# Order of the engines' work in four stages of a decoder megakernel, four buffers of expert weights, a mask product in bf16

## The chip, the cores and the metric

One core of a Trainium2 chip runs the whole program in one launch. The metric is the device time in microseconds (us). The kernel before was timed in three runs: median 4763.19, from 4760.88 to 4769.77.

## The reference

`reference()` is a decoder of four layers on `x` 32 x 128 x 128 (32 sequences of 128 tokens and 128 columns; the kernel calls a sequence a block). Each layer adds three functions of the normalised `x` to it: a self attention, a cross attention and a feed forward. The change touches four of the twelve. Cut to what matters:

```
# second self attention (L1): heads of 8 columns, 16 heads; S = 128 tokens
q, k, v = split(x @ Wproj + bproj)
Z   = k @ W0 per head
dz1 = vjp(layernorm at Z)(y1 - v)                  # the "gradient", per head and token
Z2  = Z - tril(k k^T) @ dz1;  dz2 = vjp(layernorm at Z2)(y2 - v)
ctx = q @ W0 - tril(q k^T) @ (dz1 + dz2)
ctx = group norm of ctx over tokens and columns of a head;  return ctx @ Wout + bout

# third cross attention (L2), its first part, the modulation: 128 tokens on 120 keys, 4 heads
scores = q k^T / sqrt(32), -inf where vision_mask is off
topv = top_k(scores, 32); probs = softmax(topv) scattered back
c = mean over heads(probs) @ V * text_mask
film = c @ W_film + b_film                         # scales and shifts, in and out
x = layernorm(x) * (1 + gate * scale_in) + gate * shift_in

# last self attention (L3): 16 heads of 64 columns, causal
normed = x / |x| * sqrt(dim) * gamma;  q, k, v = split(normed @ w_qkv)
return softmax(causal(q k^T / 8)) @ v @ w_out

# last feed forward (L3): product keys, 4 heads, 512 experts, 8 chosen per head
q = x @ W_q; sim = q . keys (two halves of 64 keys);  sx, sy = top_8 of each half
scores, indices = top_8(sx + sy)
w = silu((x . down_embed[indices]) * softmax(scores));  experts = sum w * up_embed[indices]
return silu(x @ W_up) @ W_down + experts
```

## The kernel before

`x` stays in SBUF for the whole program as 128 x 32 x 128 (`R.x`). Twelve stages follow each other, each a `phase` with its own buffers, PSUM tiles and semaphores. In a stage each engine (VectorE `dve`, ScalarE `act`, TensorE `pe`, GpSimd, SyncE for DMA) runs its own list of instructions, written by hand; nothing is reordered later. Engines meet through semaphores: `then_inc(s.name_ready, 1)` at a producer, `wait_ge(s.name_ready, b + 1)` at a consumer. A wait holds back everything behind it on the same engine, so the order in which an engine's list is written is part of the schedule.

The lists are software pipelines. `skewed(eng, depth, n, per)` (L180) yields rounds; in round t the code under `item(lag)` works on block (or pair of blocks) t - lag. `halved` (L201) does the same over half-blocks of eight heads. The first and last rounds are written out, those between run in a loop (`Fori`) of `per` rounds.

- **Second self attention**, `l1_attn` (L1046), 16 pairs of blocks, depth 3. A round: the normalised pair `xhat` (VectorE, L1150), its transpose `xT` (TensorE L1280, copied by ScalarE L1210), the projections `projected(b, 0)` and `projected(b, 1)` (TensorE), squares of `z` and of two later quantities (ScalarE, L1229 for the first), their reductions (VectorE L1176, L1179, L1182), the gradients, many products of TensorE, and for pair b - 3 the group norm, the transposes of ctx into `p_c`, the copy `cT` (ScalarE L1213), the output product (TensorE L1294), the sum into `x` (VectorE L1170) and the statistics of the new `x`.
- **Modulation**, `l2_film` (L2039), 32 blocks, depth 3. A round of TensorE: transpose of `xhat` (L2198), k, q and V products into `p_a`, the sum over heads of the transposed weights into `p_m` (L2209, from eight diagonal matrices `diag` that ScalarE makes at L2165 and L2166), the mask (L2215: ones times `mneg`, a row of 0 and -1e30 in a 128 x 32 x 120 f32 tile that is zero but for its first partition) and the scores into `p_s` (L2218), c (L2222), and at the end the film products L2228 to L2230. ScalarE copies film and `xr` (L2158, L2159), makes `xT`, the diagonals, the Exp and the other copies. VectorE picks the top 32 with MAX8 and match_replace.
- **Last self attention**, `l3_attn` (L2500), 64 half-blocks, depth 5. Two PSUM tiles are shared between steps: `p_x` holds by turns the heads' outputs (`av`, L2615), v, and xT; `p_y` holds q, then k (`projected`, L2602), then once per block the output projection (L2657). VectorE copies qT (L2549), eT and kT (L2558) and adds the projection to `x`.
- **Last feed forward**, `l3_ffn` (L2827), 16 pairs, depth 3. `w` holds for each pair, two rows of tokens and four heads the 512 expert weights: Exp of the sums (ScalarE L2954), times the dot products of `x` with `down` and cut to the chosen (VectorE L2904, L2911), silu (ScalarE, `silus`, L2921 and L2922; the chosen-again ones in `e_c` are summed into `rest`), the last one corrected by `added` (VectorE L2864), the sum over heads and the transpose in one go (TensorE L2979, 16 products per row of tokens), the copy `wT` (ScalarE L2940), and the product with `up` (TensorE L2991). Beside it the dense path: up (L2970), hT (ScalarE L2931), down (L2988). `w`, `sums`, `cand`, `hT` have two buffers (PER2 = 2).

## Time and profile before

The profiled execution took 4762.61 us, of which its span is 4760.8. TensorE ran at a mean granted clock of 0.812.

| | us | PE | DVE | ACT | PEclk |
|---|---|---|---|---|---|
| whole span | 4760.8 | 3486.1 | 2834.1 | 1788.2 | 0.81 |
| second self attention, 826.23 to 1385.43 | 559.20 | 314.37 | 466.45 | 65.53 | 0.73 |
| modulation, 2090.97 to 2557.13 | 466.16 | 368.50 | 294.27 | 246.62 | 0.65 |
| last self attention, 3369.99 to 3962.88 | 592.89 | 498.44 | 367.97 | 264.72 | 0.97 |
| last feed forward, 4240.03 to 4760.80 | 520.77 | 360.79 | 353.39 | 307.35 | 0.86 |

Columns PE, DVE and ACT are the busy us of TensorE, VectorE and ScalarE in the stretch. PEclk is the share of its full clock that TensorE was granted. A stretch's windows tell how full each engine is, the timeline tells in which order an engine did its work and which wait stood before it. GpSimd and the DMA queues do next to nothing in these four stages.

### The profile page before, as it was taken

What the parts mean: (1) busy time and instruction counts of PE and PEld (TensorE: products, weight loads), DVE (VectorE), ACT (ScalarE), POOL (GpSimd) and SP (SyncE); (2) the same over time, 40 slices, a digit from 0 to 9 for tenths busy, and PEclk for the clock granted to TensorE, in tenths of its full rate; (3) what the DMA queues carried; (4) which work ended last, traced back from release to release, by engine and by line L of the source; (5) the groups of instructions that cost most, each with busy time, mean ns of one, the idle gap of its engine ahead of it and who ended that gap; (6) DMA issues with size and microseconds to landing.
All of it is one profiled execution on the core that took longest, in us unless ns stands there. A gap on an engine that the chain in (4) does not pass through costs nothing. (4 is left out here: it accounts for less than half of the span.)

```text
span 4760.8 us, 71373 instructions
## 1 busy us (share of the span) xinstructions
PE 3486.1 (73%) x22142; PEld 2515.3 (53%) x22143; DVE 2834.1 (60%) x8335; ACT 1788.2 (38%) x5180; POOL 676.2 (14%) x867
## 2 busy tenths in 40 slices
PE   3576396555548858558888859999688887867776
...
DMA packets 111452, 152.49 MB, mean 32 GB/s; under 512 B 21594, under 2 KB 88216, under 8 KB 109718
## 3 DMA queue, kind: packets, MB, share of 16 engines
...
q14 instruction: 59, 0.48, 0.0%
...
## 5 line engine op out<-in xcount | busy, mean ns | idle before, releaser
L1245 PE MATMUL l_attn_p_s<-l_attn_outer,l_attn_upper 128*128 128x512 f32 x256 | 182.3, 877 | 201.9 <-DVE l_attn_outer L1190 121.4
L95 POOL TENSOR_TENSOR rstd<-vareps,minus_half 128x32 f32<-128x32 f32 x11 | 59.8, 5439 | 1527.9 <-DVE vareps L86 1393.6
L398 ACT ACTIVATE l_ffn_sg<-l_ffn_p_g 112x512 f32<-112x512 f32 x192 | 114.6, 597 | 391.9 <-PE l_ffn_p_g L378 368.5
L2582 ACT ACTIVATE l_attn_E<-l_attn_p_s,l_attn_nm 128x128 f32<-128x128 f32 x512 | 182.3, 382 | 157.6 <-DVE l_attn_nm L2545 157.6
L409 DVE TENSOR_TENSOR l_ffn_h<-l_ffn_sg,l_ffn_p_u 112x512 f32<-112x512 f32 x192 | 131.8, 687 | 172.7 <-PE l_ffn_p_u L381 172.1
L1245 PEld LDWEIGHTS l_attn_p_s<-l_attn_outer,l_attn_upper 128*128 128x128 f32 x256 | 70.2, 288 | 302.3 <-issue 178.7
L2979 PE MATMUL l_ffn_p_w<-ident,l_ffn_w 128*128 128x128 f32 x1024 | 157.0, 326 | 89.0 <-DVE l_ffn_w L2864 76.1
L381 PE MATMUL l_ffn_p_u<-l_ffn_f_xTall,l_ffn_wu 128*112 x384 | 198.3, 598 | 8.9 <-DVE l_ffn_h L409 8.9
L2979 PEld LDWEIGHTS l_ffn_p_w<-ident,l_ffn_w 128*128 128x128 f32 x1024 | 151.7, 239 | 97.1 <-DVE l_ffn_w L2864 82.4
L1404 POOL DMA_INDIRECT slots_in<-l_xattn_x,l_xattn_slot x192 | 190.0, 990 | 81.9 <-issue 50.1
L378 PE MATMUL l_ffn_p_g<-l_ffn_f_xTall,l_ffn_wg 128*112 x384 | 198.1, 597 | 0.9 <-DVE l_ffn_al L2423 0.9
L387 PEld LDWEIGHTS l_ffn_p_o<-l_ffn_wd,l_ffn_h 112*128 112x128 f32 x1536 | 176.6, 192 | 15.7 <-issue 15.7
L387 PE MATMUL l_ffn_p_o<-l_ffn_wd,l_ffn_h 112*128 112x128 f32 x1536 | 176.7, 275 | 0.0
L2602 PEld LDWEIGHTS l_attn_p_y<-l_attn_xT,l_attn_wqkv 128*128 128x128 f32 x1024 | 131.2, 194 | 42.9 <-issue 31.7
L418 DVE SCALAR_TENSOR_TENSOR x<-l_ffn_p_o,l_ffn_cw,x 128x128 f32 x256 | 85.4, 351 | 112.6 <-PE l_ffn_p_o L387 112.6
L2602 PE MATMUL l_attn_p_y<-l_attn_xT,l_attn_wqkv 128*128 128x128 f32 x1024 | 143.6, 284 | 1.6 <-DVE l_attn_qT L2549 1.6
L2209 PE MATMUL l_film_p_m<-l_film_diag,l_film_e 128*120 128x256 f32 x256 | 117.9, 641 | 34.6 <-issue 27.7
L381 PEld LDWEIGHTS l_ffn_p_u<-l_ffn_f_xTall,l_ffn_wu 128*112 128x112 f32 x384 | 68.5, 179 | 107.4 <-issue 97.6
L1210 ACT ACTIVATE l_attn_xT<-l_attn_p_t 128x256 f32<-128x256 f32 x16 | 6.1, 383 | 288.6 <-PE l_attn_p_t L1280 288.6
L2545 DVE TENSOR_REDUCE l_attn_nm<-l_attn_p_s 128x8 f32<-128x1024 f32 x64 | 78.1, 1221 | 59.6 <-PE l_attn_p_s L2626 59.6
L2582 ACT ACTIVATION_READ_ACCUMULATOR l_attn_E<-l_attn_p_s,l_attn_nm 128x1 f32 x512 | 113.4, 221 | 0.0
L378 PEld LDWEIGHTS l_ffn_p_g<-l_ffn_f_xTall,l_ffn_wg 128*112 128x112 f32 x384 | 66.5, 179 | 83.1 <-issue 82.5
...
## 6 DMA issues: line engine op xcount, KB each, us to landing
...
l_attn_toep<-kernel_rows SPq DMA_DIRECT2D x1, 8192.0 KB, 31.6
...
```

The lines of the kernel that those rows point to most:

```text
L378: pe.matmul(X.p_g[0:X.FP, k % 2], X.wg[:, w, f * X.FP:(f + 1) * X.FP], x, start=True, stop=True).then_inc(s.gate_psum, 1)
L381: pe.matmul(X.p_u[0:X.FP, k % 2], X.wu[:, w, f * X.FP:(f + 1) * X.FP], x, start=True, stop=True).then_inc(s.up_psum, 1)
L387: mm = pe.matmul(X.p_o[:, v, q * P:(q + 1) * P], X.h[:, v, f, q * P:(q + 1) * P], X.wd[:, w, f * P:(f + 1) * P], start=(f == 0), stop=(f = ...
L398: act.activation(X.sg[:, k % 2], X.p_g[0:X.FP, k % 2], ACT.Silu).then_inc(s.silu_ready, 1)
L409: dve.tensor_tensor(X.h[:, k // X.FC, k % X.FC], X.sg[:, k % 2], X.p_u[0:X.FP, k % 2], ALU.mult).then_inc(s.h_ready, 1)
L418: add = dve.scalar_tensor_tensor(out=row(R.x, b), in0=X.p_o[:, v, q * P:(q + 1) * P], scalar=weight, in1=row(R.x, b), op0=ALU.mult, op1=AL ...
L1245: mm = pe.matmul(p_s[:, r, a], upper[:], outer[:, r, a * 512:(a + 1) * 512], start=True, stop=True)
L1404: pool.indirect_dma_start(xb, bass.IndirectOffsetOnAxis(ap=slot[:, b, k:k + 1], axis=0), x6[:, u, k], None, bounds_check=last, oob_is_err= ...
L2209: mm = pe.matmul(p_m[0:SC, 0:256], e[:, u % 2, h], diag[:, h].rearrange("p k t -> p (k t)"), start=(h == 0), stop=(h == H - 1))
L2582: e = act.activation(E[:, u % 2, h], p_s[:, u % 2, odd, c * P:(c + 1) * P], ACT.Exp, bias=nm[:, u % 2, h:h + 1], accum_out=sums[:, u % 2, ...
L2602: mm = pe.matmul(p_y[:, c * P:(c + 1) * P], wqkv[:, w:w + P], xT[:, u // 2], start=True, stop=True)
L2979: mm = pe.matmul(p_w[:, c * P:(c + 1) * P], w[:, u, r, n:n + P], R.ident[:], start=(h == 0), stop=(h == H - 1))
```

## The change

Nothing is computed differently but for the type of the modulation's mask product. Per stage:

- **Second self attention.** `xhat` is made by ScalarE (Identity with scale rstd and bias shift) and no longer by VectorE. VectorE's three reductions of squares stand before the sum into `x` and the statistics of pair b - 3, no longer behind them. TensorE does both projections before the ctx transposes and the output product. ScalarE copies `cT` behind the square of `z`.
- **Modulation.** `mneg` becomes one partition of bf16, multiplied by a row of ones in bf16; the memset of the large tile goes. On TensorE the film products of a block move from the end of round item(2) to the start of the next round, item(3); the mask product stands right behind the transpose of `xhat`. On ScalarE four of the eight diagonals stand before the `xT` copy, four behind it, then the film copies, then k, q and V, and the Exp last. VectorE's film sums stand behind the top search. At the start, the semaphore `set_ready` comes in two steps and the scales `rs2` are turned in round 1.
- **Last self attention.** The output projection goes to `p_x`, and stands between the e transposes and the k products; VectorE adds it to `x` before it copies kT. The transpose of `xhat` stands before the e transposes, behind a wait for v_ready. ScalarE copies v before the Exp and `xT` between their two groups.
- **Last feed forward.** `w` has four buffers (PER_W = 4), and the loop runs over four rounds in place of two. VectorE's `added` of both rows stands behind the candidates. ScalarE: xhat, the silus of row 1, hT, xT, qT, then a wait until both silus are done, the Exp of `e_c`, then `turned` and `exps` by turns, the silus of row 0, and `x`. TensorE: `dots`, up, the transposes, q, then `heads`, `dense` and `chosen` woven with the sim products.

ScalarE's list in the last feed forward, one round (`l_ffn_w` expert weights, `l_ffn_wT` their transposed sum over heads, `l_ffn_e_c` and `l_ffn_e_t` the Exp of candidates and of the best eight). Before:

```order
L2940 ACTIVATE l_ffn_wT<-l_ffn_p_w 128x512 x2
L2942 ISA
L2942 ACTIVATE x<-l_ffn_p_x 128x256
L2944 REGISTER_ALU
L2945 ACTIVATE l_ffn_xT<-l_ffn_p_x 128x256
L2947 ACTIVATE l_ffn_qT<-l_ffn_p_q 128x1024
L2950 ACT_TABLE_LOAD
L2950 ACTIVATE l_ffn_e_c<-l_ffn_cand 128x512
L2951 ACTIVATE l_ffn_e_t<-l_ffn_cut 128x64
L2954 ACTIVATE l_ffn_w<-l_ffn_sums 128x2048
```

and after:

```order
L2970 ACTIVATE l_ffn_qT<-l_ffn_p_q 128x1024
L2976 ACT_TABLE_LOAD
L2976 ACTIVATE l_ffn_e_c<-l_ffn_cand 128x512
L2977 ACTIVATE l_ffn_e_t<-l_ffn_cut 128x64
L2948 ACTIVATE l_ffn_wT<-l_ffn_p_w 128x512
L2952 ACTIVATE l_ffn_w<-l_ffn_sums 128x2048
L2948 ACTIVATE l_ffn_wT<-l_ffn_p_w 128x512
L2951 REGISTER_ALU
L2952 ACTIVATE l_ffn_w<-l_ffn_sums 128x2048
L2942 ACT_TABLE_LOAD
L2942 ACTIVATE l_ffn_w<-l_ffn_w,l_ffn_rz 128x512
```

Both `wT` copies stood ahead of xT; now each stands ahead of one Exp of 2048 columns, and the silus follow as before.

TensorE's list in the modulation, around the end of a round (`l_film_p_f` and `l_film_p_g` the film products, `l_film_p_m` weights and c, `l_film_p_s` scores, `l_film_p_a` xT, k, q, V). Before:

```order
L2209 MATMUL l_film_p_m<-l_film_diag,l_film_e 120x256 x4
L2215 ISA
L2215 MATMUL l_film_p_s<-l_film_mneg,ones 128x120 x4
L2218 MATMUL l_film_p_s<-l_film_kq 128x120 x4
L2222 MATMUL l_film_p_m<-l_film_mT,l_film_V 128x256
L2228 MATMUL l_film_p_f<-l_film_bf,ones 128x256
L2229 MATMUL l_film_p_f<-l_film_wf,l_film_cc 128x256
L2228 MATMUL l_film_p_g<-l_film_bf,ones 128x256
L2229 MATMUL l_film_p_g<-l_film_wf,l_film_cc 128x256
L2230 MATMUL l_film_p_g<-l_film_xhat,l_film_turn 128x128
L2196 REGISTER_ALU
L2198 MATMUL l_film_p_a<-ident,l_film_xhat 128x128
```

and after:

```order
L2238 MATMUL l_film_p_m<-l_film_diag,l_film_e 120x256 x4
L2244 MATMUL l_film_p_s<-l_film_kq 128x120 x4
L2248 MATMUL l_film_p_m<-l_film_mT,l_film_V 128x256
L2202 MATMUL l_film_p_f<-l_film_bf,ones 128x256
L2203 MATMUL l_film_p_f<-l_film_wf,l_film_cc 128x256
L2202 MATMUL l_film_p_g<-l_film_bf,ones 128x256
L2203 MATMUL l_film_p_g<-l_film_wf,l_film_cc 128x256
L2217 MATMUL l_film_p_g<-l_film_xhat,l_film_turn 128x128
L2219 REGISTER_ALU
L2221 MATMUL l_film_p_a<-ident,l_film_xhat 128x128
L2227 ISA
L2227 MATMUL l_film_p_s<-l_film_mneg,l_film_onesb 128x120 x4
```

On TensorE the sequence of products is the same round a ring but for the mask product, which moves from before the scores to behind the transpose.

TensorE's list in the last self attention, the end of one half-block and the start of the next (`l_attn_p_x`, `l_attn_p_y` and `l_attn_p_e` are the PSUM tiles; the 128x512 product is v, the x4 ones q and k, the one with `headsT` the output projection). Before:

```order
L2633 MATMUL l_attn_p_x<-l_attn_wqkv,l_attn_xT 128x512
L2602 MATMUL l_attn_p_y<-l_attn_xT,l_attn_wqkv 128x128 x4
L2642 MATMUL l_attn_p_e<-ident,l_attn_E 128x128 x8
L2645 REGISTER_ALU
L2602 MATMUL l_attn_p_y<-l_attn_xT,l_attn_wqkv 128x128 x4
L2657 MATMUL l_attn_p_y<-l_attn_wout,l_attn_headsT 128x128 x8
L2615 MATMUL l_attn_p_x<-l_attn_eT,l_attn_v 64x128 x8
```

and after:

```order
L2655 MATMUL l_attn_p_x<-l_attn_wqkv,l_attn_xT 128x512
L2621 MATMUL l_attn_p_y<-l_attn_xT,l_attn_wqkv 128x128 x4
L2658 REGISTER_ALU
L2666 MATMUL l_attn_p_e<-ident,l_attn_E 128x128 x8
L2671 MATMUL l_attn_p_x<-l_attn_wout,l_attn_headsT 128x128 x8
L2621 MATMUL l_attn_p_y<-l_attn_xT,l_attn_wqkv 128x128 x4
L2632 REGISTER_ALU
L2637 MATMUL l_attn_p_x<-l_attn_eT,l_attn_v 64x128 x8
```

The output projection changes its tile and trades places with the k products.

The diff, cut to its core:

```diff
@@ l1_attn, VectorE @@
                 for item in skewed(dve, 3, PAIRS):
                     chain.restart()
-                    for b, u in item(0):
-                        pair_normalised(R, dve, b, side(xhat[:])).then_inc(s.xhat_ready, 1)
...
+                    for b, u in item(1):
+                        dve.wait_ge(s.sq2_ready, b + 1)
+                        dve.tensor_reduce(st2[:, 0], heads(t2[:]), AX.X, ALU.add).then_inc(s.var2_ready, 1)
+                    for b, u in item(2):
+                        dve.wait_ge(s.sq3_ready, b + 1)
+                        dve.tensor_reduce(gs[:, 1], heads(t3[:]), AX.X, ALU.add).then_inc(s.squares_ready, 1)
+                    for b, u in item(0):
+                        dve.wait_ge(s.sq1_ready, b + 1)
+                        dve.tensor_reduce(st1[:, 0], heads(t1[:]), AX.X, ALU.add).then_inc(s.var1_ready, 1)
                     for b, u in item(3):
                         dve.wait_ge(s.xb_ready, b + 1)
                         dve.wait_ge(s.out_psum, b + 1)
...
@@ l1_attn, ScalarE @@
                     for b, u in item(0):
+                        for r in range(2):
+                            last = act.activation(xhat[:, r * P:(r + 1) * P], row(R.x, b * 2 + r), ACT.Identity,
+                                                  scale=R.rstd[:, bass.ds(b * 2 + r, 1)], bias=R.shift[:, bass.ds(b * 2 + r, 1)])
+                        last.then_inc(s.xhat_ready, 1)
...
                         act.activation(t1[:], z[u], ACT.Square).then_inc(s.sq1_ready, 1)
+                    for b, u in item(3):
+                        act.wait_ge(s.ctxT_psum, b + 1)
+                        act.activation(cT[:], p_c[:, 0:W], ACT.Copy).then_inc(s.ctxT_ready, 1)
@@ l1_attn, TensorE @@
+                    for b, u in item(0):
+                        pe.wait_ge(s.xT_ready, b + 1)
+                        projected(b, 0)
+                    for b, u in item(0):
+                        projected(b, 1)
                     for b, u in item(3):
                         pe.wait_ge(s.ctx_ready, b + 1)
...
@@ l2_film @@
-        m4, mneg = sb("m4", [1, NB, SC // 4], U32), sb("mneg", [P, NB, SC])
+        m4, mneg, onesb = sb("m4", [1, NB, SC // 4], U32), sb("mneg", [1, NB, SC], BF16), sb("onesb", [1, P], BF16)
...
@@ l2_film, ScalarE @@
+                def diagonals(h):
+                    act.activation(diag[:, h, 0], R.ident[:], ACT.Copy, scale=rz[:, h:h + 1])
+                    return act.activation(diag[:, h, 1], turn[:], ACT.Copy, scale=rz[:, h:h + 1])
...
+                    for b, u in item(2):
+                        act.wait_ge(s.rz_ready, b + 1)
+                        diagonals(0)
+                        diagonals(1)
+                    for b, u in item(0):
+                        act.wait_ge(s.xT_psum, b + 1)
+                        act.activation(xT[:], p_a[:, 0:P], ACT.Copy).then_inc(s.xT_ready, 1)
+                    for b, u in item(2):
+                        diagonals(2)
+                        diagonals(3).then_inc(s.diag_ready, 1)
                     for b, u in item(3):
...
                         act.wait_ge(s.film_psum, b + 1)
@@ l2_film, TensorE @@
+                def film_of(out, cols, k):
+                    pe.matmul(out[:, 0:256], R.ones[0:1, :], bf[0:1, cols], start=True, stop=False)
+                    return pe.matmul(out[:, 0:256], cc[:, k * P:(k + 1) * P], wf[:, cols], start=False, stop=True)
...
+                    for b, u in item(3):
...
+                        pe.wait_ge(s.c_ready, b + 1)
+                        film_of(p_f, slice(0, 256), 1)
+                        film_of(p_g, slice(256, 512), 0)
+                        pe.matmul(p_g[:, 256:384], turn[:], xhat[:, u], start=True, stop=True).then_inc(s.film_psum, 1)
...
+                        after(pe, s.sc_ready, b)
+                        for h in range(H):
+                            pe.matmul(p_s[:, h, 0:SC], onesb[:], row(mneg, b), start=True, stop=False, skip_group_check=True)
@@ l3_attn, VectorE @@
+                    for b, hf, n, u in item(5):
+                        if hf == 1:
+                            dve.wait_ge(s.out_psum, b + 1)
+                            dve.tensor_tensor(row(R.x, b), p_x[:, 0:P], row(R.x, b), ALU.add).then_inc(s.out_taken, 1)
                     for b, hf, n, u in item(2):
                         dve.wait_ge(s.k_psum, n + 1)
@@ l3_attn, TensorE @@
                     for b, hf, n, u in item(2):
                         projected(b, hf, u, 0).then_inc(s.q_psum, 1)
+                        pe.wait_ge(s.v_ready, n + 1)
...
+                    for b, hf, n, u in item(5):
+                        if hf == 1:
+                            for c in range(2 * HC):
+                                mm = pe.matmul(p_x[:, 0:P], headsT[:, u - 1 + c // HC, c % HC], wout[:, c], start=(c == 0), stop=(c == 2 * HC - 1))
+                            mm.then_inc(s.out_psum, 1)
                     for b, hf, n, u in item(2):
                         pe.wait_ge(s.q_ready, n + 1)
                         projected(b, hf, u, 1).then_inc(s.k_psum, 1)
@@ l3_ffn @@
-    W, PAIRS, PER2 = 2 * P, NB // 2, 2
+    W, PAIRS, PER2, PER_W = 2 * P, NB // 2, 2, 4
-        w, e_c, e_t = sb("w", [P, PER2, 2, NG_]), sb("e_c", [P, PER2, 2 * H, K * K]), sb("e_t", [P, PER2, 2 * H, K])
+        w, e_c, e_t = sb("w", [P, PER_W, 2, NG_]), sb("e_c", [P, PER2, 2 * H, K * K]), sb("e_t", [P, PER2, 2 * H, K])
...
@@ l3_ffn, ScalarE @@
+                def turned(b, r):
+                    act.wait_ge(s.wT_psum, b * 2 + (r + 1))
+                    act.activation(wT[:, r].rearrange("p c t -> p (c t)"), p_w[:], ACT.Copy).then_inc(s.wT_ready, 1)
+
+                def exps(b, v, r):
+                    act.wait_ge(s.sums_ready, b * 2 + (r + 1))
+                    return act.activation(w[:, v, r], sums[:, v % PER2, r], ACT.Exp)
...
@@ l3_ffn, TensorE @@
+                def dots(b, v, r):
+                    after(pe, s.w_ready, b * 2 + (r - 1))
+                    pe.matmul(p_dot[:, r], xT[:, v % PER2, r * P:(r + 1) * P], down[:], start=True, stop=True).then_inc(s.dot_psum, 1)
+
+                def heads(b, v, r):
+                    pe.wait_ge(s.rest_added, b * 2 + (r + 1))
+                    after(pe, s.wT_ready, b * 2 + r)
...
+                def dense(b, v, r):
+                    o = p_x[:, 1, r * P:(r + 1) * P]
+                    pe.matmul(o, R.ident[:], row(R.x, b * 2 + r), start=True, stop=False)
+                    for c in range(HF):
+                        pe.matmul(o, hT[:, v % PER2, c, r * P:(r + 1) * P], wdn[:, c], start=False, stop=False)
+
+                def chosen(b, r):
+                    pe.wait_ge(s.wT_ready, b * 2 + (r + 1))
+                    for c in range(HF):
+                        mm = pe.matmul(p_x[:, 1, r * P:(r + 1) * P], wT[:, r, c], up[:, c], start=False, stop=(c == HF - 1))
+                    return mm
...
+                    for b, v in item(3):
+                        heads(b, v, 0)
+                        pe.wait_ge(s.h_ready, b + 1)
+                        for c, _ in item(4):
+                            pe.wait_ge(s.out_taken, c + 1)
+                        dense(b, v, 0)
+                        heads(b, v, 1)
```

## Rows read from the trace of the kernel before

**Rows 1.** Windows, the middle of four stages, one row each.
```profile
core 0: us, PE busy (x) PEld busy (x) DVE busy (x) ACT busy (x) POOL busy (x), PEclk, DMA share, GB/s
934.80:1345.54 410.74, 242.25 (x573) 106.12 (x572) 372.52 (x687) 51.39 (x155) 9.39 (x13) 0.77 0.00 0
2153.14:2521.52 368.38, 308.80 (x1161) 219.22 (x1161) 240.31 (x1350) 206.42 (x785) 7.09 (x25) 0.66 0.00 0
3415.01:3933.74 518.73, 451.85 (x4049) 357.98 (x4049) 336.25 (x512) 242.53 (x1091) 0.00 (x0) 1.00 0.00 0
4323.84:4692.14 368.30, 264.50 (x1656) 232.31 (x1656) 264.67 (x589) 231.14 (x457) 0.00 (x0) 0.89 0.00 0
```

**Rows 2.** Windows, last feed forward, right behind a wait of TensorE.
```profile
4446.53:4451.75 5.22, 5.22 (x24) 5.22 (x25) 5.05 (x27) 5.20 (x15) 0.00 (x0) 0.50 0.00 0
```

**Rows 3.** Timeline, last feed forward, one round, VectorE and TensorE.
```profile
start us, us, engine line op out<-in xcount [idle before <-releaser]
...
4415.66 0.17 DVE L2864 TENSOR_TENSOR l_ffn_w<-l_ffn_w,l_ffn_rest 128x4 f32<-128x4 f32 x1 [8.25 <-ACT l_ffn_e_c L2922]
...
4415.89 6.30 PE L2979 MATMUL l_ffn_p_w<-ident,l_ffn_w 128*128 128x128 f32 x32 [5.52 <-DVE l_ffn_w L2864]
...
4422.96 3.81 PE L2979 MATMUL l_ffn_p_w<-ident,l_ffn_w 128*128 128x128 f32 x32 [0.78 <-ACT l_ffn_wT L2940]
...
4432.34 1.99 PE L3004 MATMUL l_ffn_p_q<-l_ffn_xT,l_ffn_wq 128*128 128x256 f32 x8 [0.47 <-ACT l_ffn_xT L2945]
```

**Rows 4.** Timeline, last feed forward, the same round, ScalarE.
```profile
4419.31 1.00 ACT L2931 ACTIVATE l_ffn_hT<-l_ffn_p_q 128x1024 f32<-128x1024 f32 x1
4420.22 0.87 ACT L2934 ACTIVATE l_ffn_xhat<-x,shift,rstd 128x128 f32 x2
...
4431.90 0.38 ACT L2945 ACTIVATE l_ffn_xT<-l_ffn_p_x 128x256 f32<-128x256 f32 x1 [0.59 <-PE l_ffn_p_x L2998]
...
4437.39 3.69 ACT L2954 ACTIVATE l_ffn_w<-l_ffn_sums 128x2048 f32<-128x2048 f32 x2
...
4442.40 0.72 ACT L2921 ACTIVATE l_ffn_w<-l_ffn_w,l_ffn_rz 128x512 f32<-128x512 f32 x1
...
4446.19 0.70 ACT L2921 ACTIVATE l_ffn_w<-l_ffn_w,l_ffn_rz 128x512 f32<-128x512 f32 x1
```

**Rows 5.** Timeline, last self attention, TensorE.
```profile
3668.45 2.02 PE L2657 MATMUL l_attn_p_y<-l_attn_wout,l_attn_headsT 128*128 128x128 f32 x16 [0.94 <-DVE l_attn_kT L2558]
...
3671.43 0.60 PE L2621 MATMUL l_attn_p_s<-l_attn_maskb,l_attn_identb 128*128 128x512 bf16 x2
```

**Rows 6.** Windows, modulation, a later and an early round.
```profile
2303.19:2316.94 13.75, 11.78 (x43) 8.23 (x43) 8.89 (x50) 7.63 (x29) 0.28 (x1) 0.63 0.00 0
2129.97:2140.40 10.43, 7.74 (x44) 5.40 (x44) 7.06 (x43) 7.57 (x29) 0.28 (x1) 1.00 0.00 2
```

**Rows 7.** Timeline, modulation, TensorE and ScalarE.
```profile
2104.76 0.48 PE L2198 MATMUL l_film_p_a<-ident,l_film_xhat 128*128 128x128 f32 x1 [0.88 <-ACT l_film_xhat L2154]
...
2132.80 0.38 ACT L2158 ACTIVATE xattn_film<-l_film_p_g 128x256 f32<-128x256 f32 x1 [1.29 <-PE l_film_p_g L2230]
...
2133.49 0.41 ACT L2166 ACTIVATE l_film_diag<-ident,l_film_rz 128x128 f32<-128x128 f32 x1
...
2136.03 1.96 PE L2209 MATMUL l_film_p_m<-l_film_diag,l_film_e 128*120 128x256 f32 x8 [1.43 <-issue]
...
2137.82 1.05 PE L2215 MATMUL l_film_p_s<-l_film_mneg,ones 128*128 128x120 f32 x8
```

**Rows 8.** Timeline, second self attention, TensorE and VectorE.
```profile
1064.08 0.71 PE L1294 MATMUL l_attn_p_o<-l_attn_wout,l_attn_cT 128*128 128x128 f32 x4
...
1064.89 0.42 DVE L1170 TENSOR_TENSOR x<-l_attn_xb,l_attn_p_o 128x256 f32 x1
...
1066.66 0.42 DVE L1176 TENSOR_REDUCE l_attn_st<-l_attn_t 128x32 f32<-128x256 f32 x1
...
1068.81 0.42 DVE L1182 TENSOR_REDUCE l_attn_st<-l_attn_t 128x32 f32<-128x256 f32 x1 [1.41 <-ACT l_attn_t L1229]
...
1083.67 0.60 DVE L100 TENSOR_SCALAR l_attn_xhat<-x,rstd,shift 128x128 f32 x2
```

256 lines of the change are left out of this document (111 added, 145 removed).

## The prediction

> **What bounds the kernel now.** I read the windows of each stage first, because the change touches four of the twelve stages and a share over the whole span would mix limits. In the middle of the four stages [rows 1], 13 rounds of the second self attention take 410.74 us (31.6 each), 27 rounds of the modulation 368.38 (13.64), 59 half-blocks of the last self attention 518.73 (35.17 for four, 17.6 for a pair), and 12 rounds of the last feed forward 368.30 (30.69). The reader is to see which engine is nearly full: VectorE in the first (372.5 of 410.7), TensorE in the third (451.9 of 518.7, clock 1.00); in the second TensorE is busy for 308.8 of 368.4, but at a granted clock of 0.66, and in the last no engine reaches three quarters. So in the second and fourth a ring of waits sets the round. Then I read the timeline of one round engine by engine, for the wait that ends last.
>
> Last feed forward, one round [rows 2 to 4]: VectorE stands 8.25 us before `added` (L2864), which waits for the silus of row 0 on ScalarE. TensorE starts the head sums (L2979) only after it, having stood 5.52 us, and they take 6.30 us where the second set takes 3.81. ScalarE stands meanwhile, then copies, then does the Exp of the next pair, and only then the silus. It is a ring through ScalarE, VectorE and TensorE; ScalarE works 19.3 of 30.7 us (231.1 over 12 rounds, [rows 1]).
>
> Last self attention [rows 5]: per pair TensorE stands 0.94 us before the output projection (it waits for VectorE's kT copy, since both use `p_y`) and 1.43 us before the next `av` (for xT, which ScalarE copies after all its Exp).
>
> Modulation [rows 6, 7]: ring of film products, film copies and xT, eight diagonals, `p_m`, mask and scores, `p_m` again, cc. One early round ran at full clock throughout: 10.43 us. The later ones take 13.75 at 0.63.
>
> Second self attention [rows 8]: VectorE stands once, 1.41 us before the reduction L1182, which waits for ScalarE's square of z; it has spent 1.77 us just before on the add and statistics of pair b-3 (L1170 to L140).
>
> **Last feed forward: removed from the ring, and what is late next.** Four buffers of w let `heads` and `turned` of pair b-3 run while ScalarE exponentiates pair b-1, and `added` stands after VectorE's candidates. The new ring is ScalarE's own order. From the start of hT: +0.91 xT, +0.44 the q products, 1.85 later (1.99, less what their end overlaps) the head sums of row 0 (at 3.20; 3.81 long), wT at 7.05 for 0.6, first Exp 1.85 (half of 3.69) to 9.5; the head sums of row 1 start at 7.95 behind `dense` (some 0.9 of products), end at 11.8, wT to 12.4, second Exp to 14.25, a table load of about 1.3 (most of the stretch between the end of the Exp and the first silu, 4441.08 to 4442.40), silus row 0 3.79 to 19.3, x and xhat 1.2 (0.38 as for xT, and 0.87), silus row 1 3.78: 24.3 us. (3.79 is from the first silu to the one that starts row 1 [rows 4].) VectorE needs 22.06 for a round (264.7 over 12, [rows 1]) and does not set it. That is at full clock. But TensorE will have nothing from the transposes of xhat to the next xT: silus row 1 and hT, 3.78 + 0.91, about 4.6 us idle. After the present 5.52 us idle the clock is 0.50 for 5.22 us [rows 2], which costs the head sums 2.5 us (6.30 against 3.81). I take the same here, on q products and head sums, both on the ring: 24.3 + 2.7 = 27.0. So 30.7 - 27.0 = 3.7 in 13 full rounds is 48, and some 2 for the rounds at the ends: 50 us gained. Bounds: clock never falls, 24.3, so 6.4 x 13 = 83 gained; it falls and the last head sums run cold too (another 1.3), 31 gained. Loop ends fall from six to three, which I price at nothing to 1 us.
>
> **Last self attention.** The output projection moves to `p_x` and before the k products, so no product of TensorE has to wait for the kT copy any more; xT is copied between the two Exp groups. The v copy now comes before the first Exp group, which starts 0.4 us later: it is hidden, since the Exp feed only the normalisation of the next half-block, where VectorE is still busy. The new wait for v_ready on TensorE has the e transposes queued behind it; the v copy ends about 0.7 us after v_psum, beside the q products. So 0.94 goes whole; of the 1.43 about 0.35 stays, as `av` then waits for eT, which VectorE copies after qT. Per pair 17.6 - 0.94 - 1.08 + 0.1 (the add of x before kT) = 15.7; TensorE's 15.3 busy us (451.85 of 518.73 us, [rows 1]) is the floor. 31 pairs x 1.87 = 58 us gained. Bounds: 0, if v or the add stands in the way for 1.9 us per pair, and 31 x 2.3 = 71 at the floor.
>
> **Modulation.** The film products move to the start of the next round, so cc, film and the copies no longer follow one another; film and xr leave the path to the diagonals (0.69 from the first copy to the first diagonal), and only four diagonals (half of the 2.54 us up to `p_m`) follow xT, and the mask product (1.05 us, four f32 products of 120 columns) becomes bf16 on one partition, beside the wait for xT. At full clock the round of 10.43 us loses 0.69 and 1.27, and of the mask's 1.05 I count 0.2, since most of it now lies beside ScalarE's copies: 8.25 us [rows 6, 7]. The mask product is nowhere in the trace as bf16; the last self attention has two bf16 products of 512 columns in 0.60 us [rows 5], so four of 120 columns cost 0.1 to 0.6, and they lie beside the wait for xT: I take 0.3, hidden. VectorE works 8.89 us of a round [rows 6]; with 0.6 for its waits between instructions, 9.5 is a floor. The clock stretched the present ring from 10.43 to 13.64, by 31%; the same on 8.25 is 10.8, and with less f32 work on TensorE I take 10.6. 29 rounds x 3.05 = 88, and the head of the stage, where ScalarE waited for rs2 and the first transpose started at 2104.76, gives 5 [rows 7], since xhat then waits for shift alone: 93 us gained. Bounds: all rounds at the floor 9.5, 125 gained; or TensorE cold nearly throughout: its present 11.78 busy us less 1.3 for the mask product, at the present busy share of 0.86, give 12.2 a round, (13.64 - 12.2) x 29 + 5 = 47 gained.
>
> The Trainium skill (TensorE: Matmul & The Clock Gate, "Why this matters for your kernels") says that a TensorE kept busy without long pauses gets and keeps the full clock; by that the denser new round would be warm, 9.5 us. The trace speaks against it: TensorE busy 11.78 of 13.75 us still runs at 0.63 [rows 6]. The sum goes by the rows.
>
> **Second self attention: the loss.** xhat moves to ScalarE, which takes 0.51 off VectorE per round (0.60 busy, of which the next instruction overlaps 0.09). But the add and the statistics of b-3 now stand behind L1182, and out_psum comes late: TensorE does both projections before the context transposes and the output (0.55 us less in front of the second projection), so ScalarE's square of z ends at 1068.2 in place of 1068.8; cT is copied after it, to 1068.5; the output product (0.71) ends at 1069.35; then add and statistics 1.77, to 1071.2, where the gradient starts. Now it starts 0.34 behind the start of L1182, at 1069.15 [rows 8]. Per round +2.05 - 0.51 = +1.54, over 13 rounds 20, less 1.5 in the first three: 18.5 us lost. Bounds: only the 0.51 shows (8 gained), or the cold clock comes to the projections as well (30 lost).
>
> **Sum.** -50 - 58 - 93 + 18.5 = -182.5. The profiled execution took 4762.61 us (span 4760.8 and 1.8 around it), 0.6 below the median of the runs; so 4762.6 - 182.5 = 4580, as a median 4581.
>
> **Rivals.**
> - Full clock: the last feed forward and the modulation both stay warm, 33 and 32 us more gained. For it: the new rounds are denser. Against: the falls in [rows 2, 6]. 4516 us, 15%. The rule of the Trainium skill above would give this for the modulation alone: 4549.
> - TensorE-bound modulation: cold, 12.2 us a round, 46 less gained. For it: 0.63 at 11.8 busy us. Against: the warm round at 10.43 [rows 6]. 4627 us, 20%.
> - The last self attention gains nothing, because the wait for v_ready holds TensorE as long as the waits removed. For it: ScalarE copies v behind headsT. Against: the v copy fits beside the q products. 4639 us, 7%.
> - Slower: in the last self attention the clock, 1.00 over 518 us, falls as it does elsewhere. With 15.3 busy us a pair at half clock it would need up to 30.6: 31 x 13 = 400 us lost on top of the 58, so about 5040. It decides once the mean clock of that stage is under about 0.65 (23.6 us a pair). Nothing in the trace points to it, as TensorE gets denser there. 2%.
> - The forecast as laid out: 56%.
>
> The range for 8 times in 10 reaches to the full-clock case and past the cold modulation: 4512 to 4650. Differences under 0.2% (9.5 us) can't be told from no change here; all cases but the last are faster by far more: faster 0.96, same 0.01, slower 0.03.
>
> **What would show it.** After: no wait of 8 us before `added`, a round of 27 us with ScalarE the longest row and one TensorE gap of 4.6 us behind the xhat transposes; 15.7 us a pair at clock 1.00 in the last self attention, no gap before the output projection; 10.6 us a round in the modulation, p_m following the diagonals; in the second self attention two waits on VectorE, about 2.1 us before the z reduction and 0.8 before the add of x, and 33 us a round. It is wrong if the modulation stays above 12.5 us a round, or the last feed forward above 29.

## The result and the profile after

The changed kernel takes 4544.9 us (median of four runs, 4542.38 to 4549.22), the kernel before 4763.02 in the same comparison: a ratio of 0.954, with a 95% interval of 0.952 to 0.956. That is 218 us faster, where 182 were forecast; 4544.9 lies inside the range of 4512 to 4650. The profiled execution's span is 4543.5 us.

A stage begins when VectorE makes its `vareps`, so two starts give its length:

| stage | before | after | change | forecast |
|---|---|---|---|---|
| second self attention | 559.2 | 592.1 | +32.9 | +18.5 |
| modulation and the mix behind it | 654.5 | 545.5 | -109.0 | -93 |
| last self attention | 592.9 | 521.3 | -71.6 | -58 |
| last feed forward | 520.8 | 451.4 | -69.4 | -50 |
| the eight others | 2433.5 | 2433.2 | -0.3 | 0 |

All four signs are as forecast, and all four sizes are too small. The windows of the same stages, after: 12 rounds, 28 rounds, 26 blocks and 10 rounds; they answer to [rows 1]. Columns as there.

```profile
939.49:1351.61 412.12, 241.80 (x528) 106.86 (x528) 339.04 (x612) 58.11 (x169) 8.68 (x12) 0.71 0.00 0
2158.20:2446.13 287.93, 255.32 (x1093) 166.67 (x1093) 243.52 (x1403) 219.86 (x812) 7.67 (x27) 0.78 0.01 3
3373.46:3771.47 398.01, 385.80 (x3564) 313.68 (x3563) 296.95 (x457) 215.55 (x964) 0.00 (x0) 1.00 0.00 0
4180.13:4442.06 261.93, 210.80 (x1387) 186.74 (x1387) 219.84 (x491) 190.41 (x380) 0.00 (x0) 0.89 0.00 0
```

So a round takes 34.3 us in the second self attention (31.6 before), 10.28 in the modulation (13.64), 15.31 a block in the last self attention (17.6) and 26.19 in the last feed forward (30.69). In the third row TensorE is busy for 385.8 of 398.0 us: it stands for 0.47 us a block, where it stood for 2.27 before.

**Last feed forward.** The timeline after, TensorE, ScalarE and VectorE; it answers to [rows 3, 4].

```profile
4300.98 0.44 PE L3034 MATMUL l_ffn_p_x<-ident,l_ffn_xhat 128*128 128x128 f32 x2 [0.59 <-ACT l_ffn_xhat L2958]
...
4304.60 1.00 ACT L2965 ACTIVATE l_ffn_hT<-l_ffn_p_q 128x1024 f32<-128x1024 f32 x1
4304.73 0.17 DVE L2882 TENSOR_TENSOR l_ffn_w<-l_ffn_w,l_ffn_rest 128x4 f32<-128x4 f32 x1 [2.98 <-ACT l_ffn_e_c L2943]
...
4305.93 3.78 PE L3040 MATMUL l_ffn_p_q<-l_ffn_xT,l_ffn_wq 128*128 128x256 f32 x8 [4.51 <-ACT l_ffn_xT L2968]
```

and the windows of the stretch with that gap and of the one behind it (the last number but two is the granted clock):

```profile
4301.96:4305.38 3.42, 0.00 (x0) 0.00 (x0) 0.65 (x2) 3.42 (x10) 0.00 (x0) 0.80 0.00 0
4305.38:4308.79 3.41, 2.87 (x7) 2.33 (x8) 3.41 (x2) 0.49 (x2) 0.00 (x0) 0.50 0.00 0
```

The wait of 8.25 us before `added` is 2.98. TensorE has the one gap that was laid out, 4.51 us, and behind it a clock of 0.50: the q products take 3.78 us where they took 1.99 at full clock [rows 3].

**Last self attention.** TensorE after; answers to [rows 5]:

```profile
3587.77 1.95 PE L2671 MATMUL l_attn_p_x<-l_attn_wout,l_attn_headsT 128*128 128x128 f32 x16
...
3597.60 1.09 PE L2637 MATMUL l_attn_p_x<-l_attn_eT,l_attn_v 128*64 128x128 f32 x16 [0.42 <-DVE l_attn_eT L2572]
```

No wait stands before the output projection, and one of 0.42 us, for eT, before one of a block's two sets of heads' outputs (0.42 and 0.52 by turns from block to block).

**Modulation.** One round, ScalarE and TensorE; answers to [rows 7]:

```profile
2362.16 0.40 ACT L2150 ACTIVATE l_film_diag<-ident,l_film_rz 128x128 f32<-128x128 f32 x1 [0.24 <-DVE l_film_rz L2122]
...
2364.55 0.57 PE L2227 MATMUL l_film_p_s<-l_film_mneg,l_film_onesb 1*128 x4
2364.66 0.28 ACT L2170 ACTIVATE l_film_xT<-l_film_p_a 128x128 f32<-128x128 f32 x1 [1.22 <-PE l_film_p_a L2221]
...
2366.00 0.37 ACT L2178 ACTIVATE xattn_film<-l_film_p_g 128x256 f32 x1
...
2366.50 2.95 PE L2238 MATMUL l_film_p_m<-l_film_diag,l_film_e 128*120 128x256 f32 x8
```

`p_m` follows the products before it with no wait, or with one of 0.28 us in 10 of the 28 rounds (1.43 us of idle before), although half of the diagonals were made behind xT. The mask product takes 0.38 to 0.58 us in place of 1.05 or more. The rounds are of two kinds. Three that follow one another, and the wait in the third:

```profile
2353.01:2364.20 11.19, 10.58 (x41) 6.93 (x40) 8.88 (x51) 7.85 (x29) 0.28 (x1) 0.65 0.00 0
2364.20:2373.73 9.53, 9.01 (x41) 5.97 (x40) 7.48 (x42) 7.40 (x28) 0.28 (x1) 0.77 0.00 0
2373.73:2384.27 10.54, 8.16 (x41) 5.12 (x40) 9.96 (x61) 8.31 (x31) 0.28 (x1) 0.91 0.00 0
```

```profile
2380.71 0.69 PE L2202 MATMUL l_film_p_f<-l_film_bf,ones 1*128 1x256 f32 x2 [1.85 <-DVE xattn_xin L2145]
```

In 18 of the 28 rounds, at a clock of 0.65 to 0.77, TensorE waits only for the copy of c (0.47 or 0.57 us). In the other 10, at 0.91 to 0.94, it stands 1.8 us before the film products until VectorE's film sums (L2145), which now stand behind the top search, have read `p_f`; there VectorE never waits for the sums of the Exp, and sets the round.

**Second self attention.** VectorE and TensorE around the turn of a round; answers to [rows 8]:

```profile
1111.34 0.42 DVE L1173 TENSOR_REDUCE l_attn_st<-l_attn_t 128x32 f32<-128x256 f32 x1 [2.33 <-ACT l_attn_t L1230]
...
1111.71 0.71 PE L1300 MATMUL l_attn_p_o<-l_attn_wout,l_attn_cT 128*128 128x128 f32 x4 [1.28 <-ACT l_attn_cT L1233]
...
1112.67 0.42 DVE L1177 TENSOR_TENSOR x<-l_attn_xb,l_attn_p_o 128x256 f32 x1 [0.91 <-PE l_attn_p_o L1300]
...
1114.43 0.35 DVE L1128 RECIPROCAL l_attn_st<-l_attn_st 128x32 f32<-128x32 f32 x1
...
1131.05 6.35 PE L1249 MATMUL l_attn_p_s<-l_attn_outer,l_attn_upper 128*128 128x512 f32 x8 [3.82 <-DVE l_attn_part L1143]
...
1137.44 1.22 DVE L1143 TENSOR_TENSOR l_attn_part<-l_attn_p_s,l_attn_proj 128x1024 f32<-128x1024 f32 x1 [0.95 <-PE l_attn_p_s L1249]
```

The two waits are the ones forecast (2.33 and 0.91; forecast 2.1 and 0.8), and from the start of L1173 to the gradient it is 3.09 us here (3.38 in the mean of 11 rounds), 0.34 before. Not forecast is the last pair of rows: the scan on TensorE (L1249) takes 6.35 us, and VectorE now waits 0.95 for it.

### The profile page after: what moved, and what is told of

It is laid out like the page before. It is cut to its first block and busy times, and to the rows that moved or that the text cites. A ratio compares the mean times of both kernels' runs of the same rounds, so it can differ in the third digit from the quotient of the medians.

```text
span 4543.5 us, 71024 instructions
## 1 busy us (share of the span) xinstructions
PE 3398.5 (75%) x22014; PEld 2441.9 (54%) x22015; DVE 2817.2 (62%) x8303; ACT 1806.9 (40%) x5212; POOL 678.4 (15%) x867
## 5 line engine op out<-in xcount | busy, mean ns | idle before, releaser
L1249 PE MATMUL l_attn_p_s<-l_attn_outer,l_attn_upper 128*128 128x512 f32 x256 | 181.9, 876 | 204.4 <-DVE l_attn_outer L1188 131.0
L1249 PEld LDWEIGHTS l_attn_p_s<-l_attn_outer,l_attn_upper 128*128 128x128 f32 x256 | 70.2, 288 | 305.2 <-issue 185.5
L2621 PEld LDWEIGHTS l_attn_p_y<-l_attn_xT,l_attn_wqkv 128*128 128x128 f32 x1024 | 131.6, 194 | 34.1 <-issue 32.9
L3004 PEld LDWEIGHTS l_ffn_p_w<-ident,l_ffn_w 128*128 128x128 f32 x1024 | 129.8, 207 | 9.4 <-DVE l_ffn_w L2882 5.2
L3004 PE MATMUL l_ffn_p_w<-ident,l_ffn_w 128*128 128x128 f32 x1024 | 130.3, 290 | 5.9 <-DVE l_ffn_w L2882 4.2
L3040 PE MATMUL l_ffn_p_q<-l_ffn_xT,l_ffn_wq 128*128 128x256 f32 x128 | 55.6, 609 | 59.3 <-ACT l_ffn_xT L2968 59.3
L2773 ACT ACTIVATE l_xattn_E<-l_xattn_p_s 120x2048 f32<-120x2048 f32 x32 | 60.1, 1878 | 91.3 <-PE l_xattn_p_s L2819 91.3
```

The lines of the kernel that those rows point to most:

```text
L1249: mm = pe.matmul(p_s[:, r, a], upper[:], outer[:, r, a * 512:(a + 1) * 512], start=True, stop=True)
L2621: mm = pe.matmul(p_y[:, c * P:(c + 1) * P], wqkv[:, w:w + P], xT[:, u // 2], start=True, stop=True)
L3004: mm = pe.matmul(p_w[:, c * P:(c + 1) * P], w[:, v, r, n:n + P], R.ident[:], start=(h == 0), stop=(h == H - 1))
L3040: mm = pe.matmul(p_q[:, c], wq[:, c * P:(c + 1) * P], xT[:, v % PER2], start=True, stop=True)
```

## The experiments

Each kernel is the changed one with one edit, unless another start is named, so that its stage is compared with 592.1, 545.5, 521.3 and 451.4 us above. The stages are compared by their lengths and not by the whole, since the stages between the second self attention and the third, which no edit touches, took 579.3 us in the changed kernel's profile and up to 589 in others. The edited stages vary too: the second self attention took 592.1 us in the changed kernel's profile and 595.3 to 597.3 in the six others that leave it as it is (e5 to e9 and e11), so its loss may be up to 5 us larger than the 32.9 of the table.

**e1: the second self attention as before.** The whole function `l1_attn` is put back.

> The changed kernel with the second self attention as it was before, all else changed. Theory: the stages add up, and this stage alone lost 32.9 us (559.2 before, 592.1 after); so the stage takes 559 us again at 31.4 us a round and the whole 4545 - 33 = 4512 us. Rival: part of the loss in that stage is a clock that it carries over to others, or the others lose something without it; then the whole stays above 4525.

4515.16 us (4514.31 to 4524.8), stage 558.0, a round 31.7. The stages add up: the sum of the other three gains needs nothing from this one.

**e2: only xhat on ScalarE.**

```diff
 (l1_attn of before)
-                    for b, u in item(0):
-                        pair_normalised(R, dve, b, side(xhat[:])).then_inc(s.xhat_ready, 1)
...
+                act.wait_ge(s.shift_ready, 1)
...
+                        for r in range(2):
+                            last = act.activation(xhat[:, r * P:(r + 1) * P], row(R.x, b * 2 + r), ACT.Identity,
```

> As e1, but xhat of the second self attention is made by ScalarE; VectorE's, TensorE's and ScalarE's order otherwise as before. Theory: VectorE is on the path between its outer products and the second scan, so the 0.51 us that xhat took goes from each round: 30.9 us a round, stage 551, whole 4504. Rival: VectorE waits 1.3 us for the square of z at the end of each round anyway and the 0.51 only lengthens that wait: 31.4 a round, whole 4512.

4500.67 us (4494.84 to 4501.53), stage 545.0, a round 30.8: 13.1 us less than e1, about 0.96 a round where 0.51 was removed.

```profile
938.69:1308.21 369.52, 214.01 (x528) 95.31 (x528) 337.40 (x612) 58.13 (x169) 8.67 (x12) 0.78 0.00 0
```

TensorE is busy for 17.8 us a round here (214.0 over 12), 18.6 before (242.3 over 13, [rows 1]) and 20.2 in the changed kernel (241.8 over 12), for the same products: the clock is 0.78, 0.77 and 0.71. The 0.51 us that went from VectorE's path and the faster scans together make the 0.96.

**e3 and e4: VectorE's order alone, TensorE's and ScalarE's order alone.** Both start from e2.

```diff
 e3, VectorE
+                    for b, u in item(1):
+                        dve.wait_ge(s.sq2_ready, b + 1)
+                        dve.tensor_reduce(st2[:, 0], heads(t2[:]), AX.X, ALU.add).then_inc(s.var2_ready, 1)
...
                     for b, u in item(3):
                         dve.wait_ge(s.xb_ready, b + 1)
 e4, TensorE (and cT behind the square of z on ScalarE)
+                    for b, u in item(0):
+                        projected(b, 1)
                     for b, u in item(3):
                         pe.wait_ge(s.ctx_ready, b + 1)
```

> As e2, with VectorE's three reductions moved ahead of the sum into x and the statistics, as in the changed kernel; TensorE and ScalarE as in e2. Theory (VectorE's order carries the loss): the 1.77 us of sum and statistics stood in the wait for the square of z and now stand behind it, so a round takes e2's plus 1.8, about 32.7, whole e2's plus 25. Rival (TensorE's order carries it, since the output product comes late): as e2 within 0.3 us a round.

> As e2, with TensorE's and ScalarE's order of the changed kernel (both projections ahead of the context transposes and the output product, cT copied behind the square of z) and VectorE's order as before. Theory: the sum into x now waits for the output product, about 1 us behind the square of z, and 1.77 plus three reductions (1.4) stand behind it: 4 us from the square to the gradient, about 1 more than in the changed kernel, so 35.3 us a round and whole 4558. Rival (only VectorE's order matters): 31 us a round, whole 4505.

e3: 4543.74 us, stage 579.0, a round 33.5. e4: 4559.99, stage 604.7, a round 35.1. Both theories held, e3's being small (33.5 us a round against 32.7 expected). So VectorE's order alone costs 34 us of a stage, TensorE's alone 60, and both together 47 (592.1 against 545.0): the order of the reductions softens what the late output product does, and costs 34 where that product comes in time. The rows of e3 show it: nothing waits for the output product, and the sum and statistics simply stand in the way for 1.76 us, from 1106.77 to 1108.53.

```profile
1106.44 0.42 DVE L1173 TENSOR_REDUCE l_attn_st<-l_attn_t 128x32 f32<-128x256 f32 x1 [2.78 <-ACT l_attn_t L1233]
1106.77 0.41 DVE L1177 TENSOR_TENSOR x<-l_attn_xb,l_attn_p_o 128x256 f32 x1
...
1108.53 0.35 DVE L1128 RECIPROCAL l_attn_st<-l_attn_st 128x32 f32<-128x32 f32 x1
```

**e5: the mask product in f32.** `mneg` and `onesb` without BF16, one partition.

```diff
-        m4, mneg, onesb = sb("m4", [1, NB, SC // 4], U32), sb("mneg", [1, NB, SC], BF16), sb("onesb", [1, P], BF16)
+        m4, mneg, onesb = sb("m4", [1, NB, SC // 4], U32), sb("mneg", [1, NB, SC]), sb("onesb", [1, P])
```

> The changed kernel with the modulation's mask product in f32 again, still on one partition (mneg and the row of ones as f32). Theory (TensorE sets the modulation's round, being busy 8.8 of 10.3 us in the changed kernel): four f32 products cost 1.05 us at full clock against 0.38 for bf16, and about twice that in cold stretches, so a round takes 0.7 to 1.0 us more, 11.2 us, and the whole 4545 + 25 = 4570 us. Rival (the product lies in the wait for xT): under 0.2 us a round, 4545 to 4551.

4580.43 us, stage 572.6, that is 27.1 more, a round 11.12. As the theory had it: here TensorE's work sets the round. It is busy for 295.2 of 311.4 us (28 rounds) at a clock of 0.73, and none of its products waits last for VectorE's film sums, as the film products do in 10 of 28 rounds of the changed kernel.

**e6: ScalarE's order in the modulation as before.** The film copies stand ahead of xT, all diagonals behind it, the Exp before k, q and V.

```diff
+                    for b, u in item(3):
...
+                        act.activation(row(film, b), p_g[:, 0:256], ACT.Copy)
...
-                    for b, u in item(2):
-                        act.wait_ge(s.rz_ready, b + 1)
-                        diagonals(0)
-                        diagonals(1)
                     for b, u in item(0):
                         act.wait_ge(s.xT_psum, b + 1)
                         act.activation(xT[:], p_a[:, 0:P], ACT.Copy).then_inc(s.xT_ready, 1)
                     for b, u in item(2):
+                        act.wait_ge(s.rz_ready, b + 1)
+                        diagonals(0)
+                        diagonals(1)
                         diagonals(2)
                         diagonals(3).then_inc(s.diag_ready, 1)
```

> The changed kernel with ScalarE's order in the modulation as before (film copies, xT, all eight diagonals, Exp, then k, q and V); bf16 mask and the other engines as changed. Theory (ScalarE's order carries the gain): film copies stand before the diagonals again and all diagonals behind xT, about 2 us a round at full clock and more in cold stretches: 12.7 us a round against 10.3, whole 4545 + 68 = 4613 us. Rival (bf16 and VectorE's order carry it): under 11 us a round, whole under 4565.

4632.17 us, stage 617.4, that is 71.9 more, a round 12.54, clock 0.63. Taking back ScalarE's order loses two thirds of the 109 us, taking back the type of the mask a quarter. Each was taken back alone, so the two need not add up; the 10 us that neither accounts for were not tested.

**e7 and e11: the last self attention, the two halves of the change apart.** e7 puts ScalarE's order back (v behind the first Exp group, xT behind both); e11 puts TensorE's and VectorE's back (output projection in `p_y` behind the k products, with the waits for k_ready and v_ready there).

```diff
 e7, ScalarE
-                    for b, hf, n, u in item(2):
-                        act.wait_ge(s.v_psum, n + 1)
-                        act.activation(v[:, u].rearrange("p h e -> p (h e)"), p_x[:], ACT.Copy).then_inc(s.v_ready, 1)
...
 e11, TensorE
-                                mm = pe.matmul(p_x[:, 0:P], headsT[:, u - 1 + c // HC, c % HC], wout[:, c], start=(c == 0), stop=(c == 2 * HC - 1))
+                                mm = pe.matmul(p_y[:, 0:P], headsT[:, u - 1 + c // HC, c % HC], wout[:, c], start=(c == 0), stop=(c == 2 * HC - 1))
...
```

> The changed kernel with ScalarE's order in the last self attention as before (v copied between the two Exp groups, xT behind both). Theory: the wait for xT before the next heads' output comes back (1.4 us before), and the wait for v_ready on TensorE, which stands before the e transposes, is met only behind the first Exp group, up to 1.5 us in each half-block: 16.7 to 18 us a block against 15.3, whole 4545 + 45 to 85. Rival (only the freed p_y mattered): 15.3 to 15.6 us a block, whole under 4555.

> The changed kernel, but in the last self attention TensorE and VectorE stay as before (output projection in p_y behind the k products), and only ScalarE has the changed order (v copied before the Exp, xT between its two groups). Theory (the two waits are independent): the 0.94 us before the output projection stay and most of the 1.43 before the next heads' output go, 16.3 to 16.5 us a block against 17.6 before and 15.3 with both, stage near 555 us, whole 4545 + 33. Rival (xT was not the last thing that TensorE waited for, or the transpose of xhat comes too late for a place between the Exp groups and holds them up): 17.4 us or more, whole 4545 + 65.

| last self attention | ScalarE as before | ScalarE changed |
|---|---|---|
| TensorE, VectorE as before | 592.9 us, 17.6 a block | e11: 584.1, 17.3 |
| TensorE, VectorE changed | e7: 631.4, 18.8 | 521.3, 15.3 |

Each half alone gives 9 us or loses 38; together they give 72. e7 (4660.54 us) went further down than expected. In its timeline TensorE waits for v twice a block:

```profile
3701.51 0.32 PE L2662 MATMUL l_attn_p_x<-ident,l_attn_xhat 128*128 128x128 f32 x1 [1.72 <-ACT l_attn_v L2607]
...
3710.18 1.09 PE L2666 MATMUL l_attn_p_e<-ident,l_attn_E 128*128 128x128 f32 x8 [1.49 <-ACT l_attn_v L2607]
```

And e11 (4616.38 us) missed its theory, 584 where 555 was expected. The waits before the heads' outputs that were put down to xT, two blocks of the kernel before (the second is the 1.43 us of the prediction), with the copies of kT and xT ahead of the second:

```profile
3660.90 1.09 PE L2615 MATMUL l_attn_p_x<-l_attn_eT,l_attn_v 128*64 128x128 f32 x16 [1.27 <-ACT l_attn_xT L2592]
...
3677.13 0.68 DVE L2558 COPY l_attn_kT<-l_attn_p_y 128x512 f32<-128x512 f32 x1
...
3677.75 0.42 ACT L2592 ACTIVATE l_attn_xT<-l_attn_p_x,l_attn_gam 128x128 f32<-128x128 f32 x1
...
3678.55 1.09 PE L2615 MATMUL l_attn_p_x<-l_attn_eT,l_attn_v 128*64 128x128 f32 x16 [1.43 <-ACT l_attn_xT L2592]
```

and two blocks of e11:

```profile
3607.31 1.09 PE L2632 MATMUL l_attn_p_x<-l_attn_eT,l_attn_v 128*64 128x128 f32 x16 [1.43 <-DVE l_attn_kT L2575]
...
3624.28 0.98 PE L2632 MATMUL l_attn_p_x<-l_attn_eT,l_attn_v 128*64 128x128 f32 x14 [0.74 <-DVE l_attn_kT L2575]
```

The waits alternate from block to block. In every second block of the kernel before, xT's copy ended 0.10 us before the product and kT's 0.59; with xT early the wait for kT is left, 0.74 in place of 1.27. In the blocks between, the wait stays 1.43, and it was never xT's: in both kernels kT's copy ended 0.75 us before the product (xT's 0.40 before it in the kernel before, 1.02 in e11). There the end of TensorE's loop, which comes once in two blocks, lies between the wait for kT and the product; without it the product starts 0.06 us behind kT's copy. So e11 gains 0.3 us a block. In the changed kernel no wait for kT stands before the loop's end: its branch is taken at 3596.11, while the k products still run (3596.12 to 3597.18), and costs nothing that shows. Only with kT's wait gone, which the freed `p_y` does, is the earlier xT worth more.

**e8: two buffers of expert weights.** `PER_W = 2` in place of 4.

> The changed kernel with two buffers of expert weights in place of four (PER_W = 2, so that the loop is also two rounds long, with six loop ends in place of three). Theory A (as the prediction put it, four buffers let the head sums run beside the Exp): the head sums and the Exp of the same buffer wait for each other, 29 us a round or more against 26.15, whole 4545 + 37 or more. Theory B (the order alone does it, since in it each row's Exp stands behind the copy of wT, by when the head sums have read that row): 26.2 us a round, whole within 4 us of 4545.

The stage takes 450.6 us (451.4 with four), a round 26.19 in both. The whole was 4557.02; its other stages were longer. Theory B: the buffers give nothing.

**e9: the up products late.**

```diff
                     for b, v in item(2):
                         dots(b, v, 0)
-                        for c in range(HF):
-                            mm = pe.matmul(p_q[:, c], wup[:, c * P:(c + 1) * P], xT[:, v % PER2], start=True, stop=True)
-                        mm.then_inc(s.up_psum, 1)
                         dots(b, v, 1)
...
                         mm.then_inc(s.xT_psum, 1)
+                    for b, v in item(2):
...
+                        for c in range(HF):
+                            mm = pe.matmul(p_q[:, c], wup[:, c * P:(c + 1) * P], xT[:, v % PER2], start=True, stop=True)
+                        mm.then_inc(s.up_psum, 1)
                     for b, v in item(0):
                         pe.wait_ge(s.xT_ready, b + 1)
```

> The changed kernel with the up products of the last feed forward moved on TensorE from between the two dot products to behind the transposes of xhat, so that the one gap of 4.51 us before the q products becomes two of about 1.6 and 2.6 us. Theory (the gap costs twice, since the clock of 0.50 behind it stretches the q products from 1.99 to 3.78 us and the first head sums too): the clock stays near 1.00, a round takes 24.2 us against 26.15, whole 4545 - 25 = 4520. Rival (TensorE is as idle as before and the clock falls all the same, then up itself is late for hT): 26.1 to 26.8 us, whole 4545 to 4553.

The stage takes 429.7 us, 21.8 less; eight of ten rounds take 23.9 to 24.4 us, two 26.7. The ten together:

```profile
4218.24:4463.96 245.72, 196.17 (x1383) 173.44 (x1382) 220.25 (x491) 190.34 (x380) 0.00 (x0) 0.96 0.00 0
```

TensorE has the same instructions as in the changed kernel, with a clock of 0.96 against 0.89. The long rounds are those in which it fell to 0.50 all the same. The whole (4538.57, from 4526.69 to 4549.32) is blurred by the stages between, 588.9 us in its profile against 579.3.

**e10: e2 and e9 together.**

> e2 and e9 together: second self attention in its order of before with xhat on ScalarE, up products late in the last feed forward. Theory (stages add): e2's 4500.7 less what e9 gains, about 25, so 4476, a ratio of 0.940 to the kernel before. Rival (e9 gains nothing): 4501.

4481.4 us (4479.78 to 4485.08), ratio 0.9405 with an interval of 0.939 to 0.942; stages 545.0 and 429.7. They add.

**e12: the bias products of the film in two bf16 products each**, on top of e10.

```diff
+                chain(dve.tensor_copy(bfh[:], bf[0:1, :]))
+                dve.tensor_tensor(bfl[:], bf[0:1, :], bfh[:], ALU.subtract).then_inc(s.set_ready, 1)
...
-                    pe.matmul(out[:, 0:256], R.ones[0:1, :], bf[0:1, cols], start=True, stop=False)
+                    pe.matmul(out[:, 0:256], onesb[:], bfh[:, cols], start=True, stop=False)
+                    pe.matmul(out[:, 0:256], onesb[:], bfl[:, cols], start=False, stop=False)
```

> e10 with the two bias products of the modulation's film (one partition of ones times bf, 256 columns, f32, 0.63 to 0.70 us each at full clock) each in place of one f32 product as two bf16 products, of the bias rounded to bf16 and of what the rounding left. Theory (TensorE's work still sets the modulation's round, as e5 says): two bf16 products of 256 columns take about 0.3 us, so 0.7 us a round go at full clock and up to 1.0 in cold stretches: 9.5 us a round against 10.3, whole 4481 - 22 = 4459. Rival (VectorE, busy 8.5 of 10.3 us with 0.7 between its instructions, or the clock, which takes back what a less busy TensorE gives): 10.0 to 10.3 us, whole 4472 to 4481.

4472.3 us (4466.15 to 4474.81), ratio 0.9381 (0.937 to 0.939), the best of all; stage 529.1, 16.4 less, a round 9.79 against 10.28. The stage lies between the theory's 9.5 and the rival's 10.0; the whole fell by 9.1 us, to the rival's 4472, since other stages were longer (the last feed forward, the same as in e10, took 435.9 us, with three long rounds in ten and not two):

```profile
2111.87:2385.94 274.07, 223.90 (x1094) 145.46 (x1093) 243.12 (x1403) 218.16 (x815) 7.65 (x27) 0.83 0.02 5
```

VectorE is busy 8.7 of 9.79 us and TensorE 8.0. The trace points to VectorE: in 18 of the 28 rounds TensorE waits for its film sums, 29.0 of the 50.2 us that it stands, and a round at full clock looks so:

```profile
2132.57:2141.95 9.38, 6.62 (x42) 4.20 (x40) 8.85 (x53) 7.97 (x31) 0.28 (x1) 1.00 0.00 0
```

No run made VectorE faster, so what it holds back is not shown.

## Why the prediction was right, and where its sizes were off

**Last feed forward, -50 forecast, -69.4 measured.** The new ring, its one gap of 4.6 us (4.51) and the clock of 0.50 behind it came as laid out. Both terms of the round were a little too large. The full-clock round is 23.9 us where 24.3 was laid out: the rounds of e9 that run at a clock of 1.00, with the gap broken up, take that. For the clock 2.7 us were added, and the fall cost 2.3 in the mean: 1.7 in the q products (3.78, 3.78 and 3.45 by turns, against 1.99) and 0.6 in the head sums of row 0 (3.73, 4.37 and 4.85 by turns, against 3.74). 23.9 + 2.3 is 26.2, and 26.19 was measured, where 27.0 was forecast. The rounds at the ends gave 11 and not 2. One reason given was wrong: "four buffers of w let `heads` and `turned` of pair b-3 run while ScalarE exponentiates pair b-1". e8 does the same with two. In the new order each row's Exp stands behind the copy of that row's sums, when its weights have been read, so the order alone frees the buffer.

**Last self attention, -58 forecast, -71.6 measured.** The new wait for eT was forecast at 0.35 and is 0.42 or 0.52; the wait for v_ready costs nothing, as said. The working took the waits of 0.94 and 1.43 as two terms, the second for xT. They are not (e11): kT stands in both, and 1.43 was kT's wait and the loop's end in every second block, 1.27 in the others. TensorE's idle time fell from 2.27 to 0.47 us a block, by 1.80, where the sum had 1.92. The rest is busy time: 15.32 us a block before (451.85 over 29.5) and 14.84 after (385.8 over 26) for the same products. So 15.3 was no floor, and that the block takes 15.31 is chance. The forecast was near, for a sum that its parts don't bear out.

**Modulation, -93 forecast, -109 measured.** The round was forecast at 10.6 and is 10.28. The full-clock path of 8.25 was stretched by the old 31%; the clock rose from 0.66 to 0.78, and the round came out at 1.25 times 8.25. But no round shows that path: the warm ones (0.91 to 0.94) take 10.0 to 10.5 us and are held by VectorE, which the working had only as a floor of 9.5, and the cold ones take 9.5 to 11.2. That one path stretched by the clock came so near is partly luck. The head gave 4.9 us (the first transpose 8.9 us into the stage in place of 13.8), forecast 5; the first three rounds 2.6, the 28 between the fourth and the last transpose 90.8, and what follows the last transpose 10.8, of which the forecast had counted one round. By e5 and e6, 27 us hang on the mask's type and 72 on ScalarE's order. For the mask the forecast said that nothing in the trace shows it as bf16; that is so for this stage, but the second cross attention had such a product on one partition (the lines view of before, shortest, median and longest in ns):

```profile
L1587 PE MATMUL l_xattn_p_s<-l_xattn_mneg,l_xattn_onesb x64: 211/278/303, 1416.7 to 1728.4; 1*128 x40, 1*128 1x120 bf16 x24
```

The rule of the Trainium skill that was weighed with the forecast (TensorE: Matmul & The Clock Gate, "Why this matters for your kernels") was not borne out in this stage either: with 9.1 busy of 10.28 us the clock is 0.78.

**Second self attention, +18.5 forecast, +32.9 measured.** The step that failed in size is "+2.05 - 0.51" a round. By the experiments xhat on ScalarE gives 0.96 a round, and the two orders together cost 3.55 (34.34 against e2's 30.79). That more would lie between the z reduction and the gradient was forecast in its place and nearly in its size: 2.65 us more, against 2.75 in the rows shown and 3.04 in the mean. From it 0.6 was taken off, since the square of z was to end earlier. It ends 8.69 us behind the first transpose of xhat in the mean of 11 rounds, and 8.60 before: 8.15 or 8.16 in the six rounds whose projections ran at a clock of 0.95 or more, but 8.95 to 9.68 in the five at 0.78 to 0.83. The scans on TensorE are on the path too: L1249 takes 6.35 us where e2's takes 5.24, VectorE waits 0.95 for it, and from the gradient to the next transpose it is 22.35 us in the mean against e2's 21.82. The upper bound of 30 had named the cold clock, on the projections and not on the scans. With this loss 14 us larger than forecast and the three gains together 49 us larger, the errors partly cancel in the whole (217.3 us by the profiles, 182.5 forecast).

The rivals: full clock in both stages did not come (0.78, 0.89); neither did a modulation at 12.2 us, a last self attention without a gain, or a cold one.
